# Four of sixteen rounds of weight sums moved from the feed-forward part into the second batch's attention part

## The reference, cut to what matters

```
x = x + layernorm(attention(layernorm(x)))     # x: (2, 1024, 512)
x = x + layernorm(ffn(layernorm(x)))
# attention: linear, causal: state += k v^T, z += k; out = (q state) / (q z + eps); 16 heads, 4 k/v heads
# ffn: h = silu(x @ w_gate) * (x @ w_up)       # 512 -> 2048
#      keep the two largest |h| of every four, zero the others
#      h @ w_down                              # 2048 -> 512
```

## Time and profile before

| | |
|---|---|
| median of 3 runs | 1183.62 us (1183.45 to 1184.29) |
| profiled execution | 1185.25 us |
| its span in the profile | 1183.5 us |
| TensorE matmul busy | 1165.2 us, 98% |
| VectorE busy | 865.3 us, 73% |
| ScalarE, GpSimd busy | 521.2 us (44%), 414.8 us (35%) |
| mean granted TensorE clock | 0.994 |

### The profile page before, as it was taken

The page is one execution under the profiler, slowest core; times in us unless marked ns, Lnnn a source line. Parts: engine busy times, 40 slices in busy tenths (PEclk is TensorE's granted clock), DMA queues, the critical chain, the costliest instruction groups (busy, mean ns, idle before and its releaser), DMA issues.

```text
span 1183.5 us, 16279 instructions
## 1 busy us (share of the span) xinstructions
PE 1165.2 (98%) x5862; PEld 981.7 (83%) x5862; DVE 865.3 (73%) x1460; ACT 521.2 (44%) x1017; POOL 414.8 (35%) x349
## 2 busy tenths in 40 slices
PE   9999999999999999999999999999999999999996
PEld 7888888888888888888888888878888887888875
DVE  8944766656765446667566799999777879778798
ACT  5533544544545344445445544334523445333432
POOL 6421533515645225325155532132423342101013
PEclk9999999999999999999999999999999999999998
DMA  7231332322524213233235667777322566443421
GB/s 227 76 83 52 93 82 64 102 54 79 149 78 138 83 45 107 68 81 89 50 107 181 227 231 252 265 246 256 134 89 98 192 209 195 125 160 125 160 72 71
DMA packets 96367, 153.77 MB, mean 130 GB/s; under 512 B 10272, under 2 KB 31008, under 8 KB 96288
## 3 DMA queue, kind: packets, MB, share of 16 engines
q1 hardware_dynamic: 96288, 152.74, 41.5%
HBM read 96.60 MB, written 40.89 MB: 116 GB/s over the span
## 4 chain that ended last, share of the span: by engine, by line
PE 80%; DVE 15%; issue 2%; ACT 2%; DMA 1%; POOL 1%; SPq 0%; DVEq 0%; POOLq 0%
PE bank_q L804 8%; PE bank_q L806 8%; PE bank_q L805 8%; PE bank_y L806 5%; PE bank_y L805 5%; PE bank_y L804 5%; PE bank_od L1032 5%; PE bank_od L1035 4%; PE bank_t L804 3%; PE bank_t L806 3%; PE bank_t L805 3%; PE bank_s L929 2%; PE bank_od L804 2%; PE bank_od L805 2%; PE bank_od L806 2%; PE bank_s L804 2%
## 5 line engine op out<-in xcount | busy, mean ns | idle before, releaser
L804 PE MATMUL bank_q<-x_hi,w_hi 128*128 128x512 f32 x464 | 185.9, 401 | 0.3 <-ACT hidden L1340 0.3
L806 PE MATMUL bank_q<-x_lo,w_hi 128*128 128x512 f32 x464 | 181.4, 391 | 0.0
L805 PE MATMUL bank_q<-x_hi,w_lo 128*128 128x512 f32 x464 | 180.8, 390 | 0.0
L1934 POOL TENSOR_TENSOR w_lo<-stage,w_hi 128x512 fp32r<-128x512 f32 x60 | 81.2, 1361 | 209.3 <-ACT w_hi L1208 208.6
L1934 POOL TENSOR_TENSOR big_lo<-q_rows,big_hi 128x1024 fp32r<-128x1024 f32 x31 | 74.0, 2386 | 116.9 <-ACT big_hi L1247 116.9
L806 PEld LDWEIGHTS bank_q<-x_lo,w_hi 128*128 128x128 f32 x464 | 87.1, 188 | 18.8
L804 PEld LDWEIGHTS bank_q<-x_hi,w_hi 128*128 128x128 f32 x464 | 87.2, 188 | 17.2 <-issue 0.7
L805 PEld LDWEIGHTS bank_q<-x_hi,w_lo 128*128 128x128 f32 x464 | 87.4, 188 | 16.6
L806 PE MATMUL bank_y<-wout_lo,a_hi 128*128 128x512 f32 x256 | 100.0, 391 | 0.0
L804 PE MATMUL bank_y<-wout_hi,a_hi 128*128 128x512 f32 x256 | 99.8, 390 | 0.0
L805 PE MATMUL bank_y<-wout_hi,a_lo 128*128 128x512 f32 x256 | 99.8, 390 | 0.0
(11 more groups left out here) (423 smaller groups left out, 3018.3 us busy)
## 6 DMA issues: line engine op xcount, KB each, us to landing
q_rows<-scratch SPq DMA_DIRECT2D x116, 128.0 KB, 2.4
x_rows<-x SPq DMA_DIRECT2D x40, 256.0 KB, 3.0
stage<-wq SPq DMA_DIRECT2D x32, 256.0 KB, 2.8
stage<-wo SPq DMA_DIRECT2D x32, 256.0 KB, 2.8
s_keep<-x_hi SPq DMA_DIRECT2D x16, 512.0 KB, 5.1
s_keep<-x_lo SPq DMA_DIRECT2D x16, 512.0 KB, 5.8
w_hi<-s_keep SPq DMA_DIRECT2D x32, 256.0 KB, 3.4
w_lo<-s_keep SPq DMA_DIRECT2D x32, 256.0 KB, 4.2
```

Of the source, the lines that this page charges most:

```text
L804: pe.matmul(ps, whi, xhi, start=first, stop=False, skip_group_check=True)
L805: pe.matmul(ps, wlo, xhi, start=False, stop=False, skip_group_check=True)
L806: return pe.matmul(ps, whi, xlo, start=False, stop=last, skip_group_check=True)
L1934: return pool.tensor_tensor(dst, full, hi.bitcast(F32), ALU.subtract)
```

## The change

Four rounds of sums (0 to 3) are made in attention slots 31, 33, 37 and 39 of VectorE's list, behind `a_lo`. Their loads are issued in slots 29, 31, 35 and 37, their high parts made one slot later, their low parts two slots later and their stores issued three slots later. They use half 0 of `x_hi` and `x_lo`, in two new buffers (4 and 5). The other twelve rounds stay in the feed-forward part, in steps 1, 2, 5, 6, 7, 9, 10, 11, 13, 14, 15 and 17; steps 0, 12, 16 and 18 lose theirs. The first batch's rows are turned four slots later, and they wait until half 0's sums are stored.

```diff
-SUM_AT = [0, 1, 2, 5, 6, 7, 9, 10, 11, 12, 13, 14, 15, 16, 17, 18]
+SUM_IN_A = [31, 33, 37, 39]
+SUM_LD_A = [29, 31, 35, 37]
+SUM_AT = [1, 2, 5, 6, 7, 9, 10, 11, 13, 14, 15, 17]
+def sum_slot(r):
+    return SUM_AT[r - len(SUM_IN_A)]
+SUM_F = range(len(SUM_IN_A), len(SUM_IN_A) + len(SUM_AT))
 def sum_place(r):
-    return 2 + r // 2 % 2, r % 2
+    return (2 + r // 2 % 2 if r in SUM_F else 0), r % 2
 def sum_buffer(r):
     half, a = sum_place(r)
-    return 2 * (3 - half) + a
+    return 2 * (3 - half) + a if half else 4 + a
-MID_0 = [39, 42, 43, 46, 47, 50, 51, 54]
+MID_0 = [43, 46, 47, 50, 51, 54, 55, 58]
...
         def sums_kept(gate, half):
-            for buffer in ((0, 1) if half == 3 else (2, 3)):
+            for buffer in ((4, 5), (), (2, 3), (0, 1))[half]:
...
             def load_sums(r):
-                g.wait_ge(pe_q, 4 * STEPS)
-                g.wait_ge(pe_k, STEPS)
-                g.wait_ge(pe_v, B * TT)
+                uses = B if r in SUM_F else 1
+                g.wait_ge(pe_q, 2 * STEPS * uses)
+                g.wait_ge(pe_k, STEPS // 2 * uses)
+                g.wait_ge(pe_v, TT * uses)
...
+                if kind == "a":                      # SyncE
+                    for r, s in enumerate(SUM_IN_A):
+                        if s + 3 == i:
+                            store_sums(r)
+                    for r, s in enumerate(SUM_LD_A):
+                        if s == i:
+                            load_sums(r)
...
-                if job[0] == "mid" and job[1]:       # ScalarE and VectorE, split_x
+                if job[0] == "mid":
                     sums_kept(g, half)
...
+                for r, of in enumerate(SUM_IN_A):    # ScalarE, slot_a
+                    if of + 1 == s:
+                        split_sums(r)
...
+                for r, of in enumerate(SUM_IN_A):    # VectorE, end of slot_a
+                    if of + 2 == s:
+                        sum_low(r)
+                for r, of in enumerate(SUM_IN_A):
+                    if of == s:
+                        sum_weights(r)
```

More of the change, by code:

```diff
@@ L476, in build @@
         pe_g, pe_u, pe_d = sem("pe_g"), sem("pe_u"), sem("pe_d")
-        ld_s = [sem(f"ld_s{i}") for i in range(4)]
-        st_s = [sem(f"st_s{i}") for i in range(4)]
+        ld_s = [sem(f"ld_s{i}") for i in range(6)]
+        st_s = [sem(f"st_s{i}") for i in range(6)]
         dve_s1, dve_ss, act_ss, dve_sl = [sem(n) for n in ("dve_s1", "dve_ss", "act_ss", "dve_sl")]
@@ L625, in load_unit @@
                     g.wait_ge(pe_ux if side == "u" else pe_gx, count)
-                sums_kept(g, 2)
-                sums_kept(g, 3)
+                for half in (0, 2, 3):
+                    sums_kept(g, half)
                 for slot in range(8):
@@ L758, in _ @@
                             load_mid(t)
+                if kind == "a":
[5 more added lines that the diff above has]
+                            load_sums(r)
                 if kind == "f":
-                    for r in range(ROUNDS):
-                        if SUM_AT[r] + 2 == i:
+                    for r in SUM_F:
+                        if sum_slot(r) + 2 == i:
                             store_sums(r)
-                    for r in range(4, ROUNDS):
-                        if max(SUM_AT[r - 4] + 3, SUM_AT[r] - 2) == i:
+                    for r in SUM_F[4:]:
+                        if max(sum_slot(r - 4) + 3, sum_slot(r) - 2) == i:
                             load_sums(r)
@@ L780, in _ @@
                         store_piece(k)
-                for r in range(4):
-                    if tick == tick_f(0) - 2 + SUM_AT[r]:
+                for r in SUM_F[:4]:
+                    if tick == tick_f(0) - 2 + sum_slot(r):
                         load_sums(r)
@@ L1362, in slot_f @@
                     split(k)
-                for r in range(ROUNDS):
-                    if SUM_AT[r] + 1 == n:
+                for r in SUM_F:
+                    if sum_slot(r) + 1 == n:
                         split_sums(r)
@@ L1502, in split_x @@
                 g.wait_ge(act_xh, k + 1)
-                if job[0] == "mid" and job[1]:
+                if job[0] == "mid":
                     sums_kept(g, half)
@@ L1866, in slot_f @@
                     variance(job)
-                for r in range(ROUNDS):
-                    if SUM_AT[r] == n:
+                for r in SUM_F:
+                    if sum_slot(r) == n:
                         sum_weights(r)
```

## The result

The changed kernel takes 1188.26 us (median of 9 runs, 1186.18 to 1190.79) against 1184.29 us before (9 runs in the same series, 1183.45 to 1185.73). The ratio is 1.0034 with a 95% interval from 1.0023 to 1.0045: slower by a third of a per cent. The profiled execution took 1188.31 us, with a span of 1186.5 us against 1183.5.

The account below looks back on a forecast made before the run. TensorE was taken to bound the kernel, so its standstills count: -5.8 + 3.4 + 3.6 + 1.1 + 2 x 2.9 = +8.1 us on 1183.6 gave 1191.7 us, range 1178.5 to 1194.5.

Parts of the forecast that it names:

- the likeliest case: Whole kernel: step 18's gain is outweighed by three attention waits and two half clocks, 1187.5 to 1194.5 us, chance 0.4.
- the first rival: Slots 33 and 39: VectorE is not held by the query split, only slot 41's 1.1 us stays, 1178.9 us; chance 0.2.
- Step 18's wait goes with its half clock: Feed-forward step 18: TensorE's 2.91 us wait for the product into `hidden` and 2.9 us of half clock vanish, -5.8 us.
- Slot 34 waits 3.4, slot 40 3.6, slot 42 1.1 us: Attention part: work added in slots 33, 39 and 41 delays VectorE's denominators, so TensorE stands 3.4, 3.6 and 1.1 us.
- A VectorE instruction that meets a query split waits for all of it: Slots 33 and 39: VectorE waits to the end of GpSimd's query split, taken at 2.4 us, bounds 0 and 2.4.
- Slots 31, 35 and 37, SyncE, ScalarE and the transfers cost nothing: Attention part: new work in these slots is covered, and ScalarE's copies and SyncE's loads and stores delay nothing, 0 us.
- The rows turned four slots later cost nothing: First batch's rows keep their place in the eight-slot pattern, except slot 58, which takes over slot 42's; 0 us.
- Two half clocks at 2.9 us each: Behind the 3.4 and 3.6 us standstills TensorE's clock halves, costing 2 x 2.9 us, bounds 0 and 3.4 each.
- the second rival: Attention part: waits come but the half clock does not follow each; one drop 1188.8, none 1185.9 us; chance 0.22.
- The sum: Whole kernel: -5.8 + 3.4 + 3.6 + 1.1 + 2 x 2.9 = +8.1 us on the median of 1183.6.

Follow-up runs that it names:

- e1: The changed kernel with its four attention rounds (0 to 3) left out altogether, so its output differs: 1178.67 us, ratio to before 0.9957.
- e3: The changed kernel with the same four rounds at the ends of other slots, sums in 31, 32, 36 and 38: 1178.83 us, ratio to before 0.9961.
- e2: The changed kernel with GpSimd's instructions of slots 33 and 39 made on 8 columns only: 1180.25 us, ratio to before 0.9970.
- e4: The kernel before with the rounds of steps 16, 17 and 18 made one step later, nothing moved to attention: 1180.07 us, ratio to before 0.9970.
- e7: The changed kernel with six more VectorE instructions of 128x512 at the end of slot 33: 1192.73 us, ratio to before 1.0072.
- e6: e3 with rounds 2 and 3 put back where the change had them (sums in slots 37 and 39): 1184.90 us, ratio to before 1.0003.
- e5: e3 with rounds 0 and 1 put back where the change had them (sums in slots 31 and 33): 1183.36 us, ratio to before 0.9994.

## Why the prediction was right, step by step

The forecast was 1191.7 us, slower, in a range from 1178.5 to 1194.5; the measured 1188.26 lies in it, with the likeliest case's own range (1187.5 to 1194.5) around it. In rises over the kernel before, 8.1 us were forecast and 4.0 measured in the first series (1188.26 - 1184.29). The waits came where and how they were forecast; the clock did not follow them as forecast. The range is wide enough to hold the first rival's outcome as well, a faster kernel, so lying in it proves little; what bears the mechanism out is the rows and e1 to e3.

- *Step 18's wait goes with its half clock* (-5.8 forecast). Right: the product into `hidden` of step 17 starts at 798.04 and TensorE starts the up product at 801.75, so the cover is 3.0 us against 2.3. e1 gives 5.2 us for the whole feed-forward side, with step 6's 0.55 us, which was not counted, on one side and slot 60's 0.58 us more, which the prediction took at 0, on the other.
- *Slot 34 waits 3.4, slot 40 3.6, slot 42 1.1 us.* Measured 2.85, 2.60 and 0.89, and 0.25 before slot 40's scores. The order of VectorE's and GpSimd's turns was as written, instruction by instruction, and the denominator of slot 34 was within 0.2 us. From the denominator to TensorE's start it took the 1.6 us that were forecast (381.60 to 383.20). TensorE's own turn came at about 380.2 and not at 380.00, and the bracket leaves out 0.16 us, so of the forecast's 3.4 there are 3.0 by starts and 2.85 by the bracket. All together the forecast has 8.1 us, the starts 7.3, the brackets 6.6. For slot 40 the forecast left out that the delayed query split holds up TensorE's scores first (0.25 us) and so moves the time at which the quotients are wanted.
- *A VectorE instruction that meets a query split waits for all of it.* This was the unknown cost, bounded by 0 and 2.4 us and taken at 2.4. Measured: 2.58 - 0.41 = 2.2. e2 takes the instructions away and the waits go. The rule of the Trainium skill (SBUF — State Buffer, "Who interferes with whom") says the same, and the runs agree with it.
- *Slots 31, 35 and 37, SyncE, ScalarE and the transfers cost nothing.* Right: e3 equals e1.
- *The rows turned four slots later cost nothing.* Wrong, by 0.58 us in slot 60. The prediction had named slot 58 as the exception and let it go.
- *Two half clocks at 2.9 us each.* This is the step that failed, and most of the gap of 4.1 us. The profiled execution, whose time is the median's, has one half clock, of 3.4 us, which costs 1.7, and the wait of 2.60 brought none: 1.7 us in place of 5.8. Of the two places that the prediction named for a clock under 1.00, near 383 and 452, only the first has it. So what this execution shows is a form of the second rival, "one drop 1188.8" (chance 0.22 for both its forms), and not the likeliest case. The prediction reasoned that 3.4 and 3.6 us are longer than the 2.91 that had brought a half clock; the real waits were shorter than 2.91, and that row was one execution's. Its bounds, 0 and 3.4 us each, hold in the profiled executions.
- *The sum.* 8.1 - 4.1 (clock) - 0.8 (waits by starts) + 0.6 (5.2 gained in place of 5.8) = 3.8, against 4.0 measured. The upper end of the range is not worked out: with both half clocks at 3.4 us the sum gives 1192.7, and no row is named for the 1.8 us more.

## What to carry to other kernels

Work that hides behind TensorE has a price only at its place: the same four rounds cost nothing, 4.5, 6.1 or 9.6 us, by the slots at whose ends they stood. Look in each engine's timeline for the wait that is longest just ahead of the place, and ask what the next instruction is that TensorE depends on. Before putting VectorE instructions with two SBUF inputs somewhere, look at what GpSimd has to do then: the wait for one of its instructions can be added to one of them, however short that is (2.2 us to a sum of 0.41). And before moving four rounds away from a late product, try to free the step right ahead of it: e4, an edit of one table, had 3.8 us of the 5.2.

## What the runs showed of the hardware that was not expected

The half clock is not the same each time. A standstill of 2.91 us brought 6.8 us of it, one of 2.85 us 3.4 us, and one of 2.60 us in the same execution none. The one of 2.60 us in slot 40 of e7 brought none either (the clock is 1.00 from 455 to 465). In e6 a standstill of 2.59 us brought some, as this window of its slot 40 shows:

```profile
450.00:460.00 10.00, 8.77 (x36) 7.30 (x37) 3.57 (x6) 4.83 (x9) 1.28 (x1) 0.83 0.70 207
```

That is again 1.7 / 0.5 = 3.4 us at 1.2 GHz. In e7, with 7.08 us of standstill in slot 34, the same view has

```profile
380.00:395.00 15.00, 7.92 (x32) 6.40 (x31) 10.41 (x18) 5.57 (x10) 4.48 (x5) 0.77 0.40 119
```

which is 0.23 x 15 / 0.5 = 6.9 us at half speed. Here it fell at about 383.8, while TensorE still stood:

```profile
387.35 1.12 PE L946 MATMUL bank_s<-ident,scratch 128*128 128x128 f32 x4 [7.08 <-ACT scratch L1293]
```

So 3.6 us of it passed in the standstill and cost nothing, and only the rest, 3.3 us, was paid at half speed: 1.6 us, no more than the 1.7 behind the wait of 2.85 us. In the kernel before, the clock fell about 1 us before TensorE went on, in the change about 0.1 us after, in e5 and e6 0.7 to 0.8 us after.

So of three waits of 2.6 us (the change, e6, e7) one has it and two not. What decides it, no run here shows. The changed kernel's nine runs spread over 4.6 us with mean clocks from 0.992 to 0.997, and how much of that is the clock is open too, since e3, without such waits, spreads over 1.5 us and e1 over 0.4.

The mean clock of an execution is no measure of this cost. It falls at the end of every kernel here, when TensorE has nothing left to do; this is e1, in which TensorE's last matmul starts at 1166.43:

```profile
1166.80:1176.80 10.00, 0.02 (x1) 0.00 (x0) 6.95 (x16) 2.44 (x3) 4.72 (x9) 0.77 0.42 157
```
